# Six attention layers cut by halves of the tokens instead of quarters of the heads

## The reference, cut to what matters

```
for i in range(6):
    xn = adaln(x, emb, n1_w[i], n1_b[i])
    q, k, v = split(xn @ qkv_w[i].T);  q, k = rope(q), rope(k)
    x = x + attn(q, k, v) @ so_w[i].T            # scores 512 x 512, 16 heads
    xn = adaln(x, emb, n2_w[i], n2_b[i])
    q = rope(xn @ cq_w[i].T); k, v = context @ ck_w, cv_w   # 77 keys
    x = x + attn(q, k, v) @ co_w[i].T
    xn = adaln(x, emb, n3_w[i], n3_b[i])
    x = x + gelu(xn @ f1_w[i].T + f1_b[i]) @ f2_w[i].T + f2_b[i]
```

## Time and profile before

| | |
|---|---|
| median of three executions | 2410.42 us |
| the profiled execution | 2412.81 us |
| its span | 2411.0 us |
| granted TensorE clock, mean | 0.931 |
| PE, DVE, ACT, POOL busy | 86%, 64%, 53%, 10% |

### The profile page before, as it was taken

One profiled execution on the slowest core, in us unless ns is written; L12 is line 12 of the kernel. 1 busy time (PEld: TensorE's weight loads), 2 busy tenths in 40 slices (PEclk: granted clock), 3 DMA queues, 4 the chain that ended last, 5 costly groups with the idle time before them and its releaser, 6 DMA issues.

```text
span 2411.0 us, 32117 instructions
## 1 busy us (share of the span) xinstructions
PE 2076.3 (86%) x10944; PEld 913.2 (38%) x10944; DVE 1533.4 (64%) x3684; ACT 1267.0 (53%) x2430; POOL 233.7 (10%) x235
## 2 busy tenths in 40 slices
PE   7999998799999888788878887887888788868998
PEld 3444465455566422322233223323222322233433
DVE  6867576666757777467656755774667467553564
ACT  4666553477643356546636563656466556625311
POOL 0000000243320200100010001100010101020000
PEclk9999999799999989979988997999799979979999
DMA  4000000411010110001000100100110001020000
GB/s 157 1 1 1 1 1 1 137 41 40 32 56 3 47 27 1 13 15 46 1 27 1 46 1 27 40 7 1 27 46 1 25 3 28 27 84 1 1 0 9
DMA packets 43154, 61.66 MB, mean 26 GB/s; under 512 B 6097, under 2 KB 35570, under 8 KB 41586
## 3 DMA queue, kind: packets, MB, share of 16 engines
q1 hardware_dynamic: 42994, 59.61, 7.7%
HBM read 31.28 MB, written 0.52 MB: 13 GB/s over the span
## 4 chain that ended last, share of the span: by engine, by line
PE 42%; DVE 10%; ACT 9%; issue 4%; SPq 0%; POOL 0%; ACTq 0%; DMA 0%; DVEq 0%
PE ps L1969 8%; PE ps L1949 5%; ACT big L2457 4%; PE ps L1930 4%; DVE C_nm L2634 4%; PE ps L2014 3%; PE ps L2097 3%; PE ps L2204 2%; PE ps L2200 2%; PE ps L2225 2%; PE ps L2109 2%; ACT big L2537 2%; PE ps L2116 2%; PE ps L2125 2%; PE ps L2074 2%
## 5 line engine op out<-in xcount | busy, mean ns | idle before, releaser
L2634 DVE TENSOR_REDUCE C_nm<-ps 128x1 f32<-128x512 f32 x768 | 500.2, 684 | 214.3 <-PE ps L1930 211.7
L2457 ACT ACTIVATE big<-ps 128x512 f32<-128x512 f32 x768 | 427.7, 596 | 230.6 <-PE ps L1949 220.6
L1930 PE MATMUL ps<-C_attn 62*128 62x512 bf16 x768 | 277.5, 420 | 58.7 <-DVE C_nm L2634 51.1
L1949 PE MATMUL ps<-C_attn 64*128 64x512 bf16 x768 | 253.0, 396 | 64.6 <-ACT big L2457 55.4
L1969 PE MATMUL ps<-big,C_attn 128*32 128x512 f32 x1536 | 214.3, 631 | 14.4 <-ACT big L2457 14.4
L1930 PEld LDWEIGHTS ps<-C_attn 62*128 62x128 bf16 x768 | 63.3, 94 | 296.1 <-DVE C_nm L2634 157.2
L1949 PEld LDWEIGHTS ps<-C_attn 64*128 64x128 bf16 x768 | 59.2, 93 | 279.9 <-ACT big L2457 206.3
L2537 ACT ACTIVATE big<-ps,C_biasx 77x512 f32<-77x512 f32 x192 | 115.5, 678 | 56.4 <-PE ps L2101 56.3
L2390 POOL TENSOR_SCALAR lnv<-mv 128x4 f32<-128x4 f32 x36 | 8.2, 227 | 1218.0 <-DVE mv L2616 1218.0
L2596 ACT ACTIVATE big<-ps 128x512 f32<-128x512 f32 (+1 forms) x66 | 39.4, 597 | 150.0 <-PE ps L2200 149.9
L817 DVE TENSOR_REDUCE A_nm<-ps 128x2 f32<-128x1024 f32 x64 | 78.3, 1224 | 42.6 <-PE ps L631 42.2
(11 more groups left out here) (369 smaller groups left out, 3769.1 us busy)
## 6 DMA issues: line engine op xcount, KB each, us to landing
C_attn<-C_first SPq DMA_DIRECT2D x144, 128.0 KB, 2.4
...
```

What stands on the lines that cost most here:

```text
L1930: pe.matmul(ps[:, bank, :], lhsT=qs[side(hp, MAX_ROW), b, 2 * q + pq, t * P:(t + 1) * P], rhs=ks[side(hp, MAX_ROW), b, 2 * q + pq, :], sta ...
L1949: pe.matmul(ps[:, bank, :], lhsT=ks[side(1 - hp, HALF), b, 2 * q + pq, kt * P:(kt + 1) * P], rhs=qs[side(1 - hp, HALF), b, 2 * q + pq, :], ...
L2457: act.activation(prob[:, kt % 2, pq, 1 - hp, :], ps[:, bank, :], ACT.Exp, scale=SCALE)\
L2634: dve.tensor_reduce(nm[:, q % 2, t, pq, hp:hp + 1], ps[:, bank, :], AX.X, ALU.max, negate=True).then_inc(emptied[bank], 1)
```

## The change

A group of the scores is now eight heads with 256 query tokens (a half). Groups 0 and 1 are the first half of the tokens, groups 2 and 3 the second. All steps from NORM1 to FEED_BACK stand twice in the tables, once for each half, and handle two token tiles each. S is unchanged in shape and number. ST is two products of 256 columns in place of one of 512, WEIGH eight products of 256 columns in place of four of 512, ST_X and WEIGH_X likewise. Q, K, CQ and FEED put two weight blocks for one half side by side in a bank. S of a group waits for K of both halves and for Q of its own half. The GELU of a half is two pairs of products.

Memory: u (GELU's output), formerly part of `big`, becomes a tile of its own with 256 columns, so FEED_BACK of one half must be over before GELU of the next; hT exists once per batch; cT shares hT's memory; `cos` and `sin` lie interleaved by half; qx keeps its size and is written by halves; means and roots have a place for each batch and half, and most counting semaphores exist per half. New waits guard reused memory (`va`, `ks`, `cw`, `cwx`, u).

Order: all five tables are new; WINDOW is 1007.45, so a unit of the next layer stands 2014.9 places behind instead of 2428. The expert plans keep their formulas. The numbers of one step, of unit 0's column, before and now:

```
-WINDOW = 1214
+WINDOW = 1007.45
-     "FEED_BACK": [2715],          # VECTOR, unit 0
-     "STATS1": [305],
+     "FEED_BACK": [2307.81, 2681.24]},
+     "STATS1": [305.0, 671.41],
```

The core of the code's diff:

```
 def tile_of(i):
-    q, k = divmod(i, 8)
-    return q, k // 4, k % 4
+    group, k = divmod(i, 8)
+    return group, 4 * (group % 2) + k // 2, TH * (group // 2) + k % 2
...
 def scores(n, i, hp):
-    if i == 0 and hp == 0:
-        pe.wait_ge(stacked, (n + 1) * 16 * 2 * len(COMBOS))
+    if i % 16 == 0 and hp == 0:
+        pe.wait_ge(stacked_q[group // 2], (n + 1) * STACKED)
+        for g in range(2):
+            pe.wait_ge(stacked_k[g], (n + 1) * STACKED)
...
 def scores_T(n, j, hp):
-    pe.matmul(ps[:, bank, :],
-              lhsT=ks[side(1 - hp, HALF), b, 2 * q + pq, kt * P:(kt + 1) * P],
-              rhs=qs[side(1 - hp, HALF), b, 2 * q + pq, :], start=True, stop=True)\
-        .then_inc(filled[bank], 1)
+    for pq in range(2):
+        hq = 4 * e + 2 * q2 + pq
+        last = pe.matmul(ps[:, bank, cols(pq)], lhsT=ks[side(1 - hp, HALF), b, hq, kt * P:(kt + 1) * P],
+                         rhs=qs[side(1 - hp, HALF), b, hq, cols(g)], start=True, stop=True)
+    last.then_inc(filled[bank], 1)
...
 def weigh(n, i):
-    for ct in range(QUAD):
-        last = pe.matmul(ps[ct * VW:(ct + 1) * VW, PV_BANK, :], lhsT=va[:, b, kt, q * QUAD + ct, :],
-                         rhs=prob[:, kt % 2, ct // 2, ct % 2, :], start=kt == 0, stop=kt == TB - 1)
+    for q2 in range(2):
+        for ct in range(QUAD):
+            last = pe.matmul(ps[ct * VW:(ct + 1) * VW, PV_BANK, cols(q2)],
+                             lhsT=va[:, b, kt, (2 * e + q2) * QUAD + ct, :],
+                             rhs=prob[:, kt % 2, q2, ct % 2, cols(ct // 2)], start=kt == 0 and q2 == 0,
+                             stop=kt == TB - 1 and q2 == 1)
...
 # SP
+def stack(n, i, part, g):
+    dst, done = ((qs, stacked_q), (ks, stacked_k))[i]
+    if i and n >= B:
+        sp.wait_ge(pv_done, (n - B + 1) * 16)
     for r, combo in enumerate(COMBOS):
         if combo[i] == part:
-            sp.dma_start(dst[r:P:8, n % B, :, :], parts[:, i, part, :]).then_inc(stacked, 16)
+            sp.dma_start(dst[r:P:8, n % B, :, cols(g)], parts[:, i, part, cols(g)]).then_inc(done[g], 16)
...
 # ACT
-for i in hits(at["GELU"], s):
-    bank = arrived(act, ("ff", n, i))
-    act.activation(u[:, i, :], ps[:, bank, :], ACT.Gelu,
-                   bias=w[:, layer(n) % 2, LB1 + i:LB1 + i + 1]).then_inc(emptied[bank], 1)
+for k in hits(at["GELU"], s):
+    g, i = divmod(k, 2)
+    if (n or g) and i == 0:
+        arrived(act, ("f2", n, 0) if g else ("f2", n - 1, 1))
+    bank = arrived(act, ("ff", n, k))
+    for r in range(2):
+        at_row = LB1 + 2 * i + r
+        act.activation(u[:, 2 * i + r, :], ps[:, bank, cols(r)], ACT.Gelu,
+                       bias=w[:, layer(n) % 2, at_row:at_row + 1])\
+            .then_inc(emptied[bank] if r else gelu_part, 1)
...
 # memory
-u = shared[:, 0:4, :]
+u = sb("u", [P, 4, SH])
-cT = sb("cT", [P, S])
-hT = sb("hT", [P, S])
+hT = (sb("hT", [P, S]), m.hT[:, 1, :])
+cT = hT
```

More of the change, by code:

```diff
@@ L1662, in turns_aside @@
 def turns_aside(n, t):
-    return n % B == 1 and t % 2 == 1 and n < UNITS - 1
+    return ASIDE[n % B][t] and n < UNITS - 1
 D_STRIDE = 30
@@ L1673, in experts_plan @@
 def experts_plan():
-    last = [(UNITS - B + b) * WINDOW + VECTOR[b]["FEED_BACK"][0] for b in range(B)]
+    last = [(UNITS - B + b) * WINDOW + max(VECTOR[b]["FEED_BACK"]) for b in range(B)]
     plan = {"PE": [], "ACT": [], "DVE": []}
@@ L1778, in norms @@
 def norms(n, i):
[L1780 to L1782 removed]
+    return 3 * (n // B) + i + 1
 def stage_c(nc, a, m, e_b):
@@ L2185, in enter @@
+                    for k in hits(at["FEED"], s):
+                        feed(n, k)
+                    for g in hits(at["FEED_BACK"], s):
+                        feed_back(n, g)
                 def enter(b, e):
```

1181 lines of the change are left out of this document (601 added, 580 removed), and 77 rows, old and new, of tables (SCALAR, TENSOR, VECTOR).

## The result

| | before | changed |
|---|---|---|
| median | 2409.61 us (4 runs) | 2337.95 us (4 runs, 2334.39 to 2347.12) |
| ratio | | 0.971, 95% 0.9679 to 0.974 |
| profiled execution, its span | 2412.81, 2411.0 us | 2336.96, 2334.4 us |

What follows compares the result with a forecast made beforehand. Bound taken as latency of a unit's own loop, not an engine. 2412.8 + 19 (start) - 178.5 (five loops) - 25.2 (unit 10) + 3 (end) = 2231.1; median 2.4 lower: 2229 us, range 2190 to 2270.

Steps and rivals of the forecast that it cites:

- the bare stretch: Part of each layer's loop without row maxima: 57.4 us before, to become pauses of 31.6 us together.
- the 6 us for halved copies: ACT, per layer: 14 copies a unit become 28 of half length, 8.3 us at most, 6 taken.
- the halved products: PE, per layer: twice the instructions with half the columns each, 2 to 8 us, 4 taken as hidden.
- the end: Behind unit 10's last addition: unit 11's remaining work falls into the routing, 3 us added (0 to 15).
- The start's 27 us: Unit 0's first scores: forecast at about 822 us instead of 803.2, 19 us lost once (10 to 30).
- the scale: Layer loop: 92.8 ns per table place held steady, so 2014.9 places give 187.0 us, against 225.4 for 2428.
- Unit 10's 12 us: Unit 10, first scores to last addition: forecast 173 us against 198.2, 25.2 gained.
- 187 + 3: Layer loop: 187 us by places plus 3 charged for lost slack between row maxima, 190 us against 225.7.
- PE's 187.8 is not its need: PE's busy time per layer, 187.8 of 225.7 us, was said to overstate what its products need.
- The rival of the queues: Engines waiting in order at doubled steps: 10 us a layer, loop 200 us, whole 2288; chance 0.19.
- My 0 to 1 us: SP's queue, per layer: 12 stacking DMAs a unit become 24 of half size, cost 0 to 1 us.
- the rival's full clock: Layers with no stretch left at 1.2 GHz: loop 178 us, whole 2158; chance 0.12.

Runs made afterwards that it cites:

- K in one go: Changed kernel with K's six stacking transfers issued once for all 512 tokens instead of once per half; 2333.9 us, 0.968 of before.
- after_pairs_queue: Changed kernel with paired Gelus, plus two SyncE queue moves: even unit's last maxima stacked earlier, next layer's weights loaded later; 2287.1 us, 0.948 of before.

## Why the prediction was right and wrong

*Right.* The direction, and that the bare stretch would go: the longest time without a row maximum is 20.5 us, where it was to be under 25. Busy time of VectorE (139.3, about 141) and nearly that of ScalarE (138.7, about 143; without table loads it is 121.9 before and 122.8 now, so the 6 us for halved copies were 1), the loads' number (12) and length, the halved products at nothing, the end at 2 us from its term. The start's 27 us lay in its 10 to 30.

*The step that failed* is the scale: "2428 places took 225.4 us ..., 92.8 ns a place ... The new loop has 2014.9 places: 187.0 us on that scale." Taken apart, without table loads and at full clock, the loop was 210.1 us before and is 189.6 now: 86.5 ns a place before, 94.1 now. The places shrank by 17%, what TensorE has to do didn't: with the half-clock part of its busy time halved, as the prediction did for the earlier trace rows, TensorE is busy for 169.1 us of a loop before and 169.4 now (means of the four loops). By the scale these 169 us would have to fit, with every hand-over, into 174 to 177. The scale carried over the 14.5 us of low clock too, as 12.0. Unit 10's 12 us are the same step: 184.9 us for 1845 places, 100 ns each. So, against 187 + 3:

| us | in the forecast loop | measured |
|---|---|---|
| order, full clock, no loads | 174.4 + 3 | 189.6 |
| table loads | 0.5 | 6.8 |
| low clock | 12.0 | 10 |
| loop | 190 | 206.5 |

*What bounds it.* "The bound is latency, a unit's own loop, and not an engine" was half of it. "PE's 187.8 is not its need" was right, but I never set the need against the new loop. The earlier trace rows hold it: 35.6 us busy at half clock, of which 17.8 would go, leave 170. In the changed kernel 182.5 less half of 26.5 leave 169. The loop at a clock of 0.99 shows 170.96. All three are upper bounds, since the ends of products are modelled. A loop of 190 us with 12 lost to the low clock left 8 us for the waits at hand-overs, and even the loop at 0.99 has 22.5 of them (193.42 - 170.96). At equal clock, three quarters of a cut in TensorE's work came back, and 90% already in the kernel before; of an added delay in the chain 85% showed, before the change 58%. Both bind at once, ScalarE for a quarter (EXP) to 0.44 (table loads) of what is cut, VectorE for 3%.

*Table loads.* I weighed them against ScalarE's total (77% of the loop: "It fits") and not against what stands behind them. The rival of the queues had 10 us for its stops, where the loads cost 6.8; it put them down to waits ahead of copies, which fell.

*SyncE.* "Nothing else there than the maxima's stacking" was wrong, since the next layer's weights leave by the same queue, and TensorE waits for just those maxima. My 0 to 1 us agrees with what the moves and K in one go gave at equal clock (0.4 and 0.0). As run both gave 2.6 us, with less time at 1.2 GHz; why it was less isn't shown.

*The clock.* I took no gain in the sum. By the line 4.5 us of the loop's 18.7 are its gain; the rival's full clock came near only in two loops of after_pairs_queue (0.98 and 0.99), and with 193 to 195 us, not 178.
